# Another order of steps for the two local-attention layers, and fewer waits on weights

## The reference

```
xn  = layernorm(x)
out = x + gated_attention(xn) + local_layers(xn)

local_layers, twice (two layers, each with its own weights):
    h = shift_token(x)                      # second half of the channels comes from the token before
    q, k, v = split(h @ wqkv)               # 8 heads of 64
    q, k = rotary(l2norm(q) * qs, l2norm(k) * ks)
    x = x + softmax(q k^T over a window of 128) v @ wo
    h = layernorm(shift_token(x)) * lg + lb
    a, g = split(h @ w1 + b1)               # 682 + 682
    x = x + (a * gelu(g)) @ w2 + b2
```

## Time and profile before

| what | value |
|---|---|
| median of 3 runs | 1958.6 us (1950.5 to 1962.69) |
| profiled execution | 1963.61 us, its span 1961.8 us |
| mean granted TensorE clock | 0.981 |
| PE, ACT, DVE, POOL busy | 94%, 70%, 64%, 47% of the span |

### The profile page before, as it was taken

How to read it: one execution, slowest core, us unless ns; L and a number is a source line. 1 busy time by engine, 2 the same in 40 slices (tenths; PEclk the granted TensorE clock), 3 DMA queues, 4 the chain that set the end, 5 groups by cost and what they waited for, 6 DMA issues and landing times.

```text
span 1961.8 us, 47822 instructions
## 1 busy us (share of the span) xinstructions
PE 1842.9 (94%) x17808; PEld 1567.0 (80%) x17808; DVE 1246.3 (64%) x4125; ACT 1376.9 (70%) x3997; POOL 922.5 (47%) x1315
## 2 busy tenths in 40 slices
PE   6999999999999689999999999999999999999998
PEld 4788788788788469788788897887888878878777
DVE  4544543454443367777777777677777777777765
ACT  5886987878688365866757758667576585775764
POOL 2533543444344454636536446355364563654632
PEclk9999999999999889999999999999999999999999
DMA  4321320322324610110110101304112112010110
GB/s 146 99 76 56 116 87 34 116 76 77 88 78 146 196 41 23 47 55 23 47 43 24 55 15 53 122 15 166 39 39 63 34 47 65 25 54 25 44 45 28
DMA packets 127003, 128.91 MB, mean 66 GB/s; under 512 B 28112, under 2 KB 101940, under 8 KB 126772
## 3 DMA queue, kind: packets, MB, share of 16 engines
q1 hardware_dynamic: 123604, 119.56, 19.7%
q10 hardware_dynamic: 3168, 6.29, 0.9%
HBM read 72.84 MB, written 37.25 MB: 56 GB/s over the span
## 4 chain that ended last, share of the span: by engine, by line
PE 41%; DVE 11%; ACT 11%; issue 1%; POOL 1%; DMA 1%; SPq 0%; DVEq 0%; ACTq 0%; POOLq 0%
PE f_bank L1415 17%; PE f_bank L1552 7%; PE f_o_bank L1527 4%; PE f_scores L1567 4%; PE f_scores L1494 3%; ACT f_prob L1649 3%; DVE f_u L1803 3%; DVE f_gu L1799 2%; PE f_bank L1505 2%; ACT f_u L1669 2%; PE f_bank L1466 2%; PE f_bank L1509 1%; ACT f_probT L1590 1%; DVE f_actT L1688 1%; ACT f_probT L1594 1%
## 5 line engine op out<-in xcount | busy, mean ns | idle before, releaser
L594 POOL TENSOR_SCALAR a_prob<-a_prob,a_row_inv,a_gate 128x128 f32<-128x128 f32 x512 | 227.6, 468 | 377.7 <-DVE a_row_inv L932 377.7
L1370 POOL TENSOR_SCALAR f_prob<-f_prob,f_row_inv 128x192 f32<-128x192 f32 x512 | 214.5, 443 | 291.6 <-DVE f_row_inv L1745 291.6
L1415 PE MATMUL f_bank<-weights,f_actT 128*128 128x512 f32 x1152 | 302.9, 409 | 5.4 <-DVE f_norm L1693 3.9
L1552 PE MATMUL f_bank<-f_hT,f_w 128*128 128x256 f32 x2112 | 270.2, 283 | 5.4 <-DVE f_gu L1799 5.4
L1552 PEld LDWEIGHTS f_bank<-f_hT,f_w 128*128 128x128 f32 x2112 | 259.4, 189 | 10.3 <-DVE f_gu L1799 8.9
L1415 PEld LDWEIGHTS f_bank<-weights,f_actT 128*128 128x128 f32 x1152 | 211.7, 193 | 55.4 <-DVE f_norm L1693 7.7
L1352 POOL TENSOR_TENSOR f_qk_tok<-f_qk_tok,tables 128x512 f32<-128x512 f32 x128 | 165.1, 1313 | 158.4 <-DVE f_sin_part L1705 158.4
L1649 ACT ACTIVATE f_prob<-f_scores,f_neg_max 128x192 f32<-128x192 f32 x512 | 208.5, 428 | 14.1 <-DVE f_neg_max L1737 12.8
L1346 POOL TENSOR_TENSOR f_norm<-f_norm,f_minus_half 128x16 f32<-128x16 f32 x64 | 199.3, 3115 | 34.0 <-DVE f_norm L1697 32.4
L1669 ACT ACTIVATE f_u<-f_gu 128x256 fp32r<-128x256 f32 x192 | 80.3, 418 | 191.2 <-DVE f_gu L1799 191.2
L824 ACT ACTIVATE a_prob<-a_scores,a_neg_max 128x128 f32<-128x128 f32 x512 | 179.9, 392 | 24.0 <-DVE a_neg_max L923 17.0
(11 more groups left out here) (139 smaller groups left out, 3988.8 us busy)
## 6 DMA issues: line engine op xcount, KB each, us to landing
split_weights<-a_hi_lo SPq DMA_DIRECT2D x16, 512.0 KB
x_next<-states SPq DMA_DIRECT2D x32, 256.0 KB, 4.4
tables<-scaled_tables SPq DMA_DIRECT2D x16, 512.0 KB, 5.4
f_x<-states SPq DMA_DIRECT2D x16, 512.0 KB, 3.8
split_weights<-a_hi_lo SPq DMA_DIRECT2D x12, 682.0 KB
weights<-split_weights ACTq DMA_DIRECT2D x6, 1024.0 KB, 9.9
f_w<-split_weights SPq DMA_DIRECT2D x4, 1280.0 KB, 10.6
f_v_crossed<-f_v SPq DMA_DIRECT2D x40, 128.0 KB, 2.3
```

The source lines that it names most:

```text
L594: last = nc.gpsimd.tensor_scalar(part, part, row_inv[:, a % 2, head, t:t + 1], gate[:, half, t, h:h + 1], ALU.mult, ALU.mult)
L1370: last = nc.gpsimd.tensor_scalar(part, part, row_inv[:, a % 2, head, t:t + 1], 1.0, ALU.mult, ALU.mult)
L1415: last = nc.tensor.matmul(out, lhs(c, a), rhs(c, b), start=(i == 0), stop=(i == len(order) - 1))
L1552: mm = nc.tensor.matmul(out[:, which * PART:(which + 1) * PART], w1[:, wp, c, col:col + P], hT[:, hp, c, columns_of(a // FH)], start=(i == ...
```

## The change

The table `ORDER` holds the same steps in another order. On the engines this amounts to: on PE, `scores 2` comes before `transpose_x 0`, `values 0` and `values 1` before `scores 4`, `values 2` before `transpose 3`, and `transpose_qk 3` before `down 9`. On ACT, `take_o 0` (the copy of the first attention output) comes before `softmax 3`, and `load_wqkv` after `transpose_h 1` instead of at the end. On DVE, the maxima of `scores 2` come before the reciprocal of `weigh 1` and the low part of `transpose_x 0`, `take_o 0` before `weigh 3`, and `up 2` before `ln_stats 1`. On SP, `load_x` comes before `load_x1`. POOL's order stays.

Waits for weights and rows are made only where a layer opens. PE loses per sequence two waits and two increments in `project_qk` and eight waits in `project_v`; the waits for `wo`, `w1`, `w2` and the rows stay in sequences 0 and 4 alone.

```diff
-ORDER = [("softmax", 0), ("scores", 0), ("scores", 1), ("weigh", 0), ("weigh", 1), ("softmax", 1), ("load_x1", 0), ("transpose_x", 0),
-         ("scores", 2), ("transpose", 0), ("softmax", 2), ("transpose", 1), ("load_x", 0), ("scores", 3), ("weigh", 2), ("project_qk", 0),
-         ("weigh", 3), ("softmax", 3), ("rope", 0), ("scores", 4), ("values", 0), ("values", 1), ("take_o", 0), ("transpose", 2),
-         ("project_qk", 1), ("scores", 5), ("weigh", 4), ("rope_sum", 0), ("softmax", 4), ("transpose", 3), ("project_qk", 2),
-         ("values", 2), ("scores", 6), ("weigh", 5), ("load_tables", 0), ("load_others", 0), ("shift_keys", 0), ("rope", 1), ("softmax", 5),
...
-         ("shift_back", 0), ("up", 10), ("up", 11), ("down", 7), ("down", 8), ("cross_values", 0), ("down", 9), ("add_attended", 0),
-         ("transpose_qk", 3), ("down", 10), ("down", 11), ("out", 0), ("out", 1), ("load_wqkv", 0)]
+ORDER = [("softmax", 0), ("softmax", 1), ("scores", 0), ("scores", 1), ("weigh", 0), ("scores", 2), ("weigh", 1), ("transpose_x", 0),
+         ("transpose", 0), ("softmax", 2), ("transpose", 1), ("scores", 3), ("weigh", 2), ("project_qk", 0), ("load_x", 0), ("take_o", 0),
+         ("softmax", 3), ("values", 0), ("values", 1), ("load_x1", 0), ("weigh", 3), ("rope", 0), ("scores", 4), ("transpose", 2),
+         ("project_qk", 1), ("softmax", 4), ("scores", 5), ("weigh", 4), ("rope_sum", 0), ("values", 2), ("transpose", 3),
+         ("project_qk", 2), ("softmax", 5), ("scores", 6), ("values", 3), ("weigh", 5), ("rope", 1), ("transpose_qk", 0), ("take_o", 1),
...
+         ("down", 0), ("down", 1), ("project_v", 3), ("up", 3), ("down", 2), ("transpose_h", 1), ("cross_values", 0), ("rope", 3),
+         ("load_wqkv", 0), ("up", 4), ("down", 3), ("up", 5), ("up", 6), ("up", 7), ("down", 4), ("up", 8), ("up", 9), ("rope_sum", 3),
+         ("down", 5), ("down", 6), ("transpose_qk", 2), ("up", 10), ("up", 11), ("x1_bias", 0), ("down", 7), ("down", 8),
+         ("add_attended", 0), ("transpose_qk", 3), ("down", 9), ("out", 0), ("out", 1), ("down", 10), ("down", 11)]
...
+        LAYER_STARTS = (0, BATCH)
...
                     if a % TILES == 0:
-                        pe.wait_ge(kept.weights_loaded[QUERY], loads(1, layer))
-                        pe.sem_inc(pe_carried, 1)
+                        if fresh:
+                            pe.wait_ge(kept.weights_loaded[QUERY], loads(1, layer))
+                            pe.sem_inc(pe_carried, 1)
...
                 elif kind == "project_v":
-                    pe.wait_ge(kept.weights_loaded[2], loads(1, layer))
+                    if fresh:
+                        pe.wait_ge(kept.weights_loaded[2], loads(1, layer))
...
-                    prepare(it, kind, a, next_layer if a // PER_CHUNK[kind] == HALVES - 1 else layer)
+                    ahead = a // PER_CHUNK[kind] == HALVES - 1
+                    prepare(it, kind, a, next_layer if ahead else layer, ahead and it == BATCH - 1)
...
-                        if a == 0:
+                        if a == 0 and it in LAYER_STARTS:
                             pe.wait_ge(w1_loaded, loads(4, layer))
```

More of the change, by code:

```diff
@@ new lines @@
+ORDER = [("softmax", 0), ("softmax", 1), ("scores", 0), ("scores", 1), ("weigh", 0), ("scores", 2), ("weigh", 1), ("transpose_x", 0),
[3 more added lines that the diff above has]
+         ("project_qk", 2), ("softmax", 5), ("scores", 6), ("values", 3), ("weigh", 5), ("rope", 1), ("transpose_qk", 0), ("take_o", 1),
+         ("transpose", 4), ("scores", 7), ("softmax", 6), ("weigh", 6), ("project_qk", 3), ("project_o", 0), ("rope_sum", 1), ("weigh", 7),
+         ("transpose", 5), ("softmax", 7), ("load_tables", 0), ("load_others", 0), ("shift_keys", 0), ("shift_front", 0), ("shift_back", 0),
+         ("take_o", 2), ("values", 4), ("values", 5), ("transpose", 6), ("project_v", 0), ("transpose_qk", 1), ("transpose", 7),
+         ("ln_stats", 0), ("ln_apply", 0), ("take_o", 3), ("rope", 2), ("values", 6), ("values", 7), ("project_v", 2), ("transpose_h", 0),
+         ("project_o", 1), ("rope_sum", 2), ("up", 0), ("up", 1), ("up", 2), ("project_v", 1), ("ln_stats", 1), ("ln_apply", 1),
+         ("down", 0), ("down", 1), ("project_v", 3), ("up", 3), ("down", 2), ("transpose_h", 1), ("cross_values", 0), ("rope", 3),
+         ("load_wqkv", 0), ("up", 4), ("down", 3), ("up", 5), ("up", 6), ("up", 7), ("down", 4), ("up", 8), ("up", 9), ("rope_sum", 3),
+         ("down", 5), ("down", 6), ("transpose_qk", 2), ("up", 10), ("up", 11), ("x1_bias", 0), ("down", 7), ("down", 8),
+         ("add_attended", 0), ("transpose_qk", 3), ("down", 9), ("out", 0), ("out", 1), ("down", 10), ("down", 11)]
@@ L1384, in iteration @@
                         if a == 0:
-                            pool.wait_ge(rows_loaded, loads(1, layer))
+                            if it in LAYER_STARTS:
+                                pool.wait_ge(rows_loaded, loads(1, layer))
                             pool.wait_ge(edge_kept.sem, edge_kept.past(it, ("shift_keys", 0)))
@@ L1432, in transpose_part, with prepare @@
                 last.then_inc(filled.sem, 1)
-            def prepare(it, kind, a, layer):
+            def prepare(it, kind, a, layer, fresh):
                 if kind == "transpose_x":
@@ L1443, in prepare @@
                     if a % TILES == 0:
-                        pe.wait_ge(kept.weights_loaded[QUERY], loads(1, layer))
-                        pe.sem_inc(pe_carried, 1)
+                        if fresh:
+                            pe.wait_ge(kept.weights_loaded[QUERY], loads(1, layer))
+                            pe.sem_inc(pe_carried, 1)
                         pe.wait_ge(emptied.sem, emptied.past(it, ("transpose_x", a // TILES), CT - 1))
                     for which in (QUERY, KEY):
-                        if which == KEY and a % TILES == 0:
+                        if which == KEY and a % TILES == 0 and fresh:
                             pe.wait_ge(kept.weights_loaded[KEY], loads(1, layer))
```

2 lines of the change are left out of this document (1 added, 1 removed).

## The result

The changed kernel takes 1986.4 us in the median of 4 runs (1981.8 to 1989.1), the kernel before 1958.8 us beside it. The ratio is 1.0148, 95% interval 1.0131 to 1.0166: **slower by 1.5%**, where I had forecast 1950 us and a range up to 1963. The profiled execution has a span of 1983.7 us and the same mean clock as before, 0.981.

The account below looks back on a forecast made before the run. PE, busy 94% of the span, was taken as the bound. Terms +4.5 - 9.1 - 3.9 - 3.0 = -11.5 us gave 1952.1 us for the profiled execution; the median was forecast at 1950 us, range 1943 to 1963.

Parts of the forecast that it names:

- hidden by 0.5 us on POOL: Middle of a chunk: `softmax 3` ends later, yet 0.5 us before POOL's `weigh 3` needs it; uncovered, up to 1.1 us per chunk.
- the term of -3.9 us: Middle of a chunk: moving `values 2` ahead removes PE's wait before `project_qk 2`, 15 times, 3.9 us in all.
- Rival E: Middle: `softmax 3` comes too late for POOL in each of 15 chunks, 16.5 us on top of the forecast, 1966 us; chance 0.06.
- The opening: Start of a chunk: the maxima of `scores 2` delay DVE's low part, +0.3 us each without a drop, 15 times, +4.5 us.
- POOL hides the later reciprocal: Start of a chunk: the later reciprocal of `weigh 1` costs nothing because POOL is still busy with `weigh 0`.
- The drops: PE's clock falling at openings: ten at 1.23 us before, eight at 0.4 us after, on work with slack; -9.1 us.
- the switch of layers: Weight loads issued some 15 us earlier no longer delay the store, so that chunk gets its usual length: -3.0 us.
- The middle's gain: Middle of a chunk: `values 2` ahead of `transpose 3` gives DVE 1.05 us to free the bank; -3.9 us.
- Tail and waits removed: Reordered end steps and dropped waits on PE: bound 0 to -3 us over all, taken as 0.
- The rule cited for the price of low time: Throttled time times one minus the clock ratio: 1.57 us per drop at an opening; the sum used 1.23.
- rival D: Openings: the one long gap before `scores 2` makes all 14 drop at 1.23 us each, 1965 us; chance 0.12.

Follow-up runs that it names:

- e2: The kernel before with only the changed order of the middle of a chunk: 1975.2 us, ratio 1.0091.
- e12: The changed kernel with `take_o 0` put back behind `softmax 3` and `scores 4`: 1969.3 us, ratio 1.0046 against before.
- e9: The kernel before with `scores 2` ahead of `transpose_x 0` on PE alone, DVE's order as before: 1959.9 us, ratio 1.0000.
- e1: The kernel before with only the changed order of the opening, on PE and DVE: 1965.2 us, ratio 1.0036.
- e7: The kernel before with the changed opening, but the reciprocal of `weigh 1` back ahead of the maxima of `scores 2`: 1967.5 us, ratio 1.0039.
- e8: The kernel before with 17 unused transposes of the identity added per opening in PE's idle time: 1954.9 us, ratio 0.9972.
- e11: The changed kernel with 17 unused transposes ahead of `scores 2` and 6 ahead of the second part of `transpose 0`: 1988.3 us, ratio 1.0141 against before.
- e6: The kernel before with one move, `values 2` ahead of `transpose 3` on PE: 1962.9 us, ratio 1.0006.
- e3: The kernel before with everything of the change but opening and middle, `load_x1` ahead of `load_x` as before: 1956.6 us, ratio 0.9990.
- e10: The kernel before with unused transposes at the openings, earlier weight loads, fewer waits and the changed tail: 1948.4 us, ratio 0.9943.
- e14: The kernel before with POOL's power for the keys left out, so it computes something else: 1956.3 us, ratio 0.9986.

## Why the prediction was wrong

**The step that failed** is "hidden by 0.5 us on POOL" in the middle of a chunk, with the term of -3.9 us that rests on it. For `weigh 3` itself it was right: in e2 `weigh 3` starts 16.85 us after the opening, 16.84 before. What I didn't ask is what stands behind it. DVE takes the reciprocal of `weigh 3`, then `rope 0` and the next sums of squares, all in order, and the reciprocal comes 1.46 us later in e2's chunk at 1420.91 (1.0 us in first halves, as at 1663.01). So DVE's work falls beside other instructions of POOL. In that chunk `weigh 3` takes 2.05 us instead of 1.63, the second power starts 0.41 us later, and `weigh 6` meets DVE's `rope_sum` and takes 3.62 instead of 1.66; the power behind it, which met `rope_sum` before, gives back 1.08 (2.90 instead of 3.98). In first halves `weigh 4` (2.27 instead of 1.65) takes the place of `weigh 3`. POOL pauses for 0.2 us in all from the first power to `weigh 7`, so all of it is paid: that stretch takes 28.0 us instead of 26.6, and 27.5 instead of 25.7 in first halves. POOL's 47% on the page is a mean over a stretch of full load and one of nearly none. The price is 20 us of the changed kernel's 29 (e12).

Rival E, to which I gave 0.06, had the right step and by luck nearly the right price, 16.5 us. Its mechanism, `softmax 3` too late for POOL, didn't happen.

**The opening**, forecast +0.3 us, is +0.78. The cause was the one named, the maxima ahead of the low part (e9 against e1), but I stopped at the first bank. On the rows after, the second part of `transpose 0` is 0.35 us late, and then `transpose 1` waits 0.21 us for a `weigh 1` that started 0.77 us late; "POOL hides the later reciprocal" was false. Putting the reciprocal ahead alone doesn't help (e7): the first projection starts at 9.65 us there, later still.

**The drops** came out in the profiled executions. Those of the kernel before cost 0.9 to 1.6 us, near the 1.23 taken for each, and the eight after cost 2.5 us together, 0.3 each where I took 0.4. That there are eight was a guess that came true. They have the slack that I named, PE waits for DVE's low part anyway. But it is there only because the maxima make the low part late, so it is paid for in the opening's 0.78 us: with DVE's order kept, drops cost 0.7 to 1.2 (e9). For the median the term was too large: filling the gaps of the old kernel is worth 5.5 us (e8), or some 7 without the longer switch chunk. I can't say why. The mean clock of the other runs beside e8 is 0.981 in the median, that of the profiled execution, so fewer drops in them don't explain it. In the changed kernel filling gains nothing that the interval would show (e11).

Put together for the profiled execution, 15 chunks longer by 2.1 to 2.4 us (one by 0.7), less about 9 us of drops and 3 us for the switch of layers, make up the 22 us of span to within 2 us.

**The middle's gain** of 3.9 us for `values 2` was a wait moved, not removed, and in second halves the move costs 1.1 us (e6). **The switch of layers** was right: chunk 79.07 instead of 82.03 (e3), and 5.9 us where the opening before it has no drop (e10 against e8). **Tail and waits removed** at nothing: nothing contradicts it; the time of e3 bounds both and the switch together to between -0.28% and +0.08%.

The rule cited for the price of low time (1.57 us a drop) is an upper end of what the runs show: 0.9 to 1.6 us at the old opening, 0 to 0.7 at the changed one, 0.7 to 1.2 in e9. What fills the low time, and what would hold up PE anyway, decides. The Trainium skill's warning against waits between bursts ("TensorE: Matmul & The Clock Gate", Loop structure matters more than you think), as rival D read it, would have had the long gap cost; with DVE's order kept the kernel takes the time of before (e9).

## What to carry to other kernels

Before moving a step ahead of another on one engine, look in the timelines for an engine, besides the one that bounds the kernel, that goes long without an idle bracket; its busy share over the whole span doesn't show it. Here POOL, at 47%, was just in time: relieving it gained nothing (e14), but each us by which it ended later made the chunk nearly 1 us longer, however much slack a single instruction seemed to have. Ask then not only when the moved step's next reader starts, but which instructions the whole queue behind it will now run beside. A wait that is taken away in front of such a chain came back behind it (e6). Idle time of PE that can't be removed can be filled with transposes whose result isn't used, to hold the clock: together with the earlier weight loads that was worth 0.57% here (e10), though nothing in the changed kernel (e11).

## What the runs showed of the hardware

POOL's four multiplications of `weigh` take 1.62 us alone and 3.61 us beside DVE's addition and product of 128x1024 (1.22 and 1.25 us); a power takes 2.91 us alone and 3.98 beside the same, so it loses half as much. The other way, DVE's small maximum (L1702) over 128x16 takes 0.17 us alone and up to 1.32 us beside POOL's rotary product. Here is DVE's timeline in the kernel after, beside the `weigh 6` of POOL's timeline above (1459.00 to 1462.61):

```profile
1459.74 1.22 DVE L1717 TENSOR_TENSOR f_qk_tok<-f_qk_tok,f_sin_part 128x1024 f32<-128x1024 f32 x1
1461.07 1.25 DVE L1720 TENSOR_TENSOR f_qk_tok<-f_qk_tok,f_norm 128x1024 f32<-128x1024 f32 x1
```

The Trainium skill ("SBUF — State Buffer", Who interferes with whom) says that VectorE and GpSimd share one pair of ports under an exclusive lock, and that a VectorE instruction with two inputs in SBUF contends with a GpSimd instruction that reads SBUF. By that rule the delay is at most the length of DVE's operations, and the trace agrees: 3.61 - 1.62 = 1.99 us for `weigh` and 3.98 - 2.91 = 1.07 us for the power, beside some 2.47 us. So moving a step changes what POOL's instructions take, not only when they start.
